# A two-layer network kernel on one core: loads of x moved to another queue in its first stage, loads and first products reordered in its last ones

## What is computed

```python
x = x + _L0_conv_ref(_ln_c(x), ...)   # involution: 7x7 taps, dilation 2, 8 groups, taps made per point from a reduction of _ln_c(x)
t = t + _L0_ffn_ref(_ln_t(t), ...)    # 16 spectral filters; weights of four matrix sets mixed by a softmax of 4 values
x = x + _L1_conv_ref(_ln_c(x), ...)   # 3x3 convolution of rank one, its factors made from means of the image
t = t + _L1_ffn_ref(_ln_t(t), ...)    # 8 experts, the two best of a softmax per point
# _ln_c, _ln_t: (v - mean) / sqrt(var + eps) over the 128 channels of a point
# inside _L0_ffn_ref:
y_soft = softmax(log_weights + gumbel); weights = one_hot(argmax(y_soft)) - y_soft + y_soft
```

## Time and profile before

| what | us |
|---|---|
| median of three runs (2830.85 to 2849.27) | 2848.44 |
| the profiled execution, its own time | 2834.71 |
| its span, first to last instruction | 2832.9 |
| `normalise_in`, to the next block's first GpSimd instruction | 0 to 207.0 |
| `back_and_norm`, first instruction | 2160.5 |
| `experts`, first instruction | 2376.9 |

### The profile page before, as it was taken

The page is one execution under the profiler, slowest core; times in us unless marked ns, Lnnn a source line. Parts: engine busy times, 40 slices in busy tenths (PEclk is TensorE's granted clock), DMA queues, the critical chain, the costliest instruction groups (busy, mean ns, idle before and its releaser), DMA issues. The chain is left out here.

```text
span 2832.9 us, 78733 instructions
## 1 busy us (share of the span) xinstructions
PE 2358.3 (83%) x34528; PEld 1799.9 (64%) x34528; DVE 1495.8 (53%) x3482; ACT 1309.7 (46%) x2623; POOL 366.5 (13%) x651
## 2 busy tenths in 40 slices
PE   3549898768169999999999999999785984799898
PEld 2328898633058888888888888888433751344444
DVE  3852433357136665666566566656211452576777
ACT  3443433356046655665566565656210563333332
POOL 1311111124300000000000000000021001122211
PEclk7676977879689999999999999999897886899999
DMA  6457535365621111111101111110398410000000
GB/s 196 144 138 162 107 82 102 73 216 177 153 77 45 45 45 45 45 45 45 36 23 44 45 45 45 45 23 19 123 298 290 140 55 13 13 20 25 21 24 26
DMA packets 155227, 235.09 MB, mean 83 GB/s; under 512 B 18310, under 2 KB 112623, under 8 KB 151372
## 3 DMA queue, kind: packets, MB, share of 16 engines
q1 hardware_dynamic: 122392, 134.74, 16.4%
q0 software_dynamic: 32496, 95.33, 12.5%
HBM read 141.68 MB, written 88.31 MB: 81 GB/s over the span
## 5 line engine op out<-in xcount | busy, mean ns | idle before, releaser
L1026 DVE COPY spc_g<-spc_pz 128x512 f32<-128x512 f32 x1024 | 629.1, 682 | 306.5 <-PE spc_pz L922 306.5
L996 ACT ACTIVATE spc_g<-spc_pz 128x512 f32<-128x512 f32 x1024 | 549.2, 612 | 284.5 <-PE spc_pz L922 284.1
L922 PE MATMUL spc_pz<-spc_v,spc_as 108*128 108x128 bf16 x8192 | 553.9, 219 | 13.8 <-issue 1.7
L922 PEld LDWEIGHTS spc_pz<-spc_v,spc_as 108*128 108x128 bf16 x8192 | 473.6, 97 | 102.7 <-ACT spc_g L996 31.4
L943 PE MATMUL spc_pz<-spc_g,spc_u 128*20 128x128 f32 x16384 | 469.2, 274 | 21.4 <-DVE spc_g L1026 17.3
L943 PEld LDWEIGHTS spc_pz<-spc_g,spc_u 128*20 128x20 f32 x16384 | 451.4, 134 | 47.5 <-ACT spc_g L996 30.1
L1533 PE MATMUL moe_ex<-moe_ew,moe_d 128*128 128x512 f32 x512 | 249.8, 611 | 32.8 <-DVE moe_yt L1690 32.4
L907 PE MATMUL spc_pu<-spc_f,spc_s 128*128 128x256 f32 x768 | 207.6, 396 | 80.6 <-DMA spc_s<-s_sf 80.6
L1690 DVE SCALAR_TENSOR_TENSOR moe_yt<-moe_ex,moe_gb,moe_yt 128x128 f32<-128x128 f32 x768 | 209.6, 343 | 103.3 <-ACT moe_yt L1592 98.0
L566 DVE SCALAR_TENSOR_TENSOR inv_xo<-inv_pa,inv_mask,inv_xo 128x256 f32<-128x256 f32 x256 | 123.6, 484 | 219.7 <-PE inv_pa L524 187.0
L544 ACT ACTIVATE inv_b<-inv_pb 112x1024 f32<-112x1024 f32 x128 | 125.5, 1021 | 216.8 <-PE inv_pb L503 216.8
(11 more groups left out here) (218 smaller groups left out, 2282.0 us busy)
## 6 DMA issues: line engine op xcount, KB each, us to landing
s_yd<-spc_yo SPq DMA_DIRECT2D x128, 160.0 KB
s_sf<-fwd_so SPq DMA_DIRECT2D x16, 1024.0 KB, 6.4
spc_s<-s_sf POOLq DMA_DIRECT2D x32, 512.0 KB, 6.1
ivs_y<-s_yd POOLq DMA_DIRECT2D x32, 512.0 KB, 5.1
s_td<-ivs_to SPq DMA_DIRECT2D x32, 512.0 KB, 5.3
ln_t<-s_td SPq DMA_DIRECT2D x32, 512.0 KB, 3.9
lnc_xc<-in_x SPq DMA_DIRECT2D x32, 256.0 KB, 5.3
s_xn<-lnc_xn SPq DMA_DIRECT2D x64, 128.0 KB
```

The costliest lines, as they stand in the source:

```text
L922: m = pe.matmul(pz[:, (p + 2) % 3, e // 4, 2 * FT * (e % 4):2 * FT * (e % 4) + 2 * FT], AS[:, x, 8 * p + e, :], V[:, k, x, :, FT * t:FT * ...
L996: act.activation(g_out(p, 0), g_in(p, 0), ACT.Copy).then_inc(ga, 1)
L1026: v.tensor_copy(g_out(p, 1), g_in(p, 1)).then_inc(gd, 1)
```

## The change

In `normalise_in` x gets six buffers, and its loads move from SP's list to GpSimd's, where the other work of that list is put between them. SP's list begins with the small constants and both first matrix sets, and the other sets go out one DMA at a time behind the stores of chunks 3 to 8. The square root, the normalisation, the turning back, the product and its removal move one step later each, the product has four banks, and the weight work lies at other steps. In `back_and_norm` the loads of X of images 1 to 3 wait for units of the image before. In `experts` the first group's neighbour rows are issued first, from GpSimd and ACT, and its products use four banks each and an order of their own.

```diff
-    NQ, D = NB * NCH, 4
+    NQ, D, DX = NB * NCH, 4, 6
-        pr = A.ps("pr", [P, 2, CH])
+        pr = A.ps("pr", [P, 4, CH])
-            for s in range(NQ + 5):
+            for s in range(NQ + 7):
...
+            for q in range(NQ):
+                if q >= DX:
+                    pool.wait_ge(x_turned, q - DX + 1)
+                pool.dma_start(xc[:, q % DX, :], xv[q // NCH, q % NCH]).then_inc(x_in[q % DX], 16)
+                if q == 0:
+                    step(pool.memset(eps[:], EPS_C))
+                if q == 3:
+                    step(pool.memset(zero[:], 0.0))
+                if q in (17, 18):
+                    if q == 17:
+                        pool.wait_ge(mats_used, 4)
+                    combine(q - 17)
+                if 19 <= q < 23:
+                    split(q - 19)
+                if 8 <= q < 17:
+                    store_zeros(q - 8)
+                if q == 24:
+                    pool.wait_ge(wc_ready, 1)
+                    pool.dma_start(S["D2M"], d2[:].rearrange("p a b -> p (a b)")).then_inc(out_done, 16)
+                if q == 26:
+                    store_parts(1)
             store_parts(0)
-            store_parts(1)
...
             sp.dma_start(ident[:], I["ident"]).then_inc(const_in, 16)
-            load_x(0)
+            sp.dma_start(lg[:, 0, :], I["lw"].partition_broadcast(P)).then_inc(small_in, 16)
+            sp.dma_start(lg[:, 1, :], I["gum"].partition_broadcast(P)).then_inc(small_in, 16)
+            sp.dma_start(sg[:, 0, :], I["sigma"].partition_broadcast(P)).then_inc(small_in, 16)
+            sp.dma_start(prio[:], I["prio"]).then_inc(small_in, 16)
             sp.dma_start(wr[:], I["w_reduce"]).then_inc(const_in, 16)
             sp.dma_start(rbias[:], I["b_reduce"]).then_inc(const_in, 16)
...
-            load_mats(0)
+            for i in range(2):
+                for m in range(3):
+                    load_mats(i, m)
             for q in range(NQ):
                 b, n = divmod(q, NCH)
-                if q + D < NQ:
-                    load_x(q + D)
                 sp.wait_ge(xn_ready, q + 1)
...
-                if q in (1, 6, 9):
-                    load_mats((1, 6, 9).index(q) + 1)
+                if 3 <= q < 9:
+                    load_mats(2 + (q - 3) // 3, q % 3)
...
-                if q >= 2:
-                    pe.wait_ge(red_ready, q - 1)
-                pe.matmul(pr[:, q % 2], wr[:], xnc[:, q % 2], start=True, stop=True).then_inc(reduced, 1)
+                if q >= 4:
+                    pe.wait_ge(red_ready, q - 3)
+                pe.matmul(pr[:, q % 4], wr[:], xnc[:, q % 2], start=True, stop=True).then_inc(reduced, 1)
...
-                if live(s - 3):
-                    turn_back(s - 3)
                 if live(s - 4):
-                    reduction(s - 4)
+                    turn_back(s - 4)
+                if live(s - 5):
+                    reduction(s - 5)
...
-                q = s - 1
+                q = s - 2
                 if live(q):
                     act.wait_ge(mv_ready, q + 1)
...
-                q = s - 2
+                q = s - 3
...
-                q = s - 3
+                q = s - 4
...
-                elif s in (5, 8, 11, 14):
-                    add_mats((5, 8, 11, 14).index(s))
-                elif s == 10:
+                elif s in (3, 5, 9, 12):
+                    add_mats((3, 5, 9, 12).index(s))
+                elif s == 7:
                     inverse_weights()
-                elif s in (16, 18):
-                    combine(s // 2 - 8)
-                elif s in (20, 22, 24, 26):
-                    split(s // 2 - 10)
+                elif s in (14, 16):
+                    combine(s // 2 - 7)
+                elif s in (18, 20, 22, 24):
+                    split(s // 2 - 9)
...
-                if live(s - 1):
-                    scales(s - 1)
-                if live(s - 5):
-                    take(s - 5)
+                if live(s - 2):
+                    scales(s - 2)
+                if live(s - 6):
+                    take(s - 6)
...
             for b in range(NB):
+                if b:
+                    pool.wait_ge(x_done, NU * (b - 1) + 2)
                 pool.dma_start(X[:, T * b:T * b + T], S["X1C"][b]).then_inc(x_in[b], 16)
...
+        def conv_at(i, c):
+            return pd[:] if i else ex[:, c]
+
+        def centre_at(i, c):
+            return (pd[:], pf[:, 0], pf[:, 1], pl[:])[0 if i else c]
...
+            sp.dma_start(cmat[:], I["cmat"]).then_inc(early_in, 16)
...
-            pool.memset(eb[:], 0.0).then_inc(set_up, 1)
+            for tap in range(0, 9, 2):
+                neighbour(pool, 0, tap, v9_in[0])
             pool.memset(rw[:], 0.0).then_inc(set_up, 1)
             pool.memset(eps[:], EPS_T).then_inc(set_up, 1)
             pool.memset(onec[:], 0.0).then_inc(set_up, 1)
+            pool.memset(eb[:], 0.0).then_inc(set_up, 1)
...
-            pe.wait_ge(const_in, 16 * (6 + GT))
+            pe.wait_ge(early_in, 80)
+            conv(0, 0)
+            for c in range(1, GC):
+                conv(0, c)
+                centre(0, c - 1)
+            centre(0, GC - 1)
             pe.wait_ge(set_up, 5)
-            for c in range(GC):
-                conv(0, c)
-                centre(0, c)
+            pe.wait_ge(const_in, 16 * (5 + GT))
...
-            act.wait_ge(set_up, 5)
+            for tap in range(1, 9, 2):
+                neighbour(act, 0, tap, early_in)
             for c in range(GC):
                 centred(0, c)
+            act.wait_ge(set_up, 5)
...
-            v.wait_ge(const_in, 16 * (6 + GT))
             for c in range(GC):
                 add_conv(0, c)
+            v.wait_ge(const_in, 16 * (5 + GT))
```

More of the change, by code:

```diff
@@ L145, in store_parts, with split @@
                         "e (k d) -> e k d", k=KX)).then_inc(out_done, 16)
[L147 to L153, removed]
+            def split(k):
+                if k == 0:
+                    step(pool.tensor_copy(parts[:, 1, 0], ab[:, 1]))
+                elif k == 1:
+                    step(pool.tensor_tensor(tmp[:, 1], ab[:, 1], parts[:, 1, 0], ALU.subtract))
+                elif k == 2:
+                    step(pool.tensor_copy(parts[:, 1, 1], tmp[:, 1]))
+                else:
+                    step(pool.tensor_tensor(parts[:, 1, 2], tmp[:, 1], parts[:, 1, 1], ALU.subtract))
+                    pool.sem_inc(parts_ready[1], 1)
@@ new lines, in store_zeros @@
+            def store_zeros(k):
+                if k == 8:
+                    pool.dma_start(S["VP"], zero[0:66, 0:NB * 66].rearrange("h (b w) -> h b w", b=NB)).then_inc(out_done, 16)
+                    return
+                side, k = (0, HP - PADH)[k // 4], k % 4
+                if k == 3:
+                    pool.dma_start(S["XN"][side:side + PADH].rearrange("h x w b y c -> (h x w b y c)").rearrange("(p m) -> p m", m=2048),
+                                   zero[0:PADH * HP, :]).then_inc(out_done, 16)
+                else:
@@ L161, in _ @@
-            split3(pool, ab[:, 1], tmp[:, 1], parts[:, 1, 0], parts[:, 1, 1], parts[:, 1, 2], step)
-            pool.sem_inc(parts_ready[1], 1)
+            xv = I["x"].rearrange("b c (n m) -> b n c m", m=CH)
+            for q in range(NQ):
[19 more added lines that the diff above has]
+                    store_parts(1)
@@ L168, in _, with load_mats @@
         def _(sp):
[L169 to L176, removed]
+            def load_mats(i, m):
                 if i >= 2:
                     sp.wait_ge(mats_used, i - 1)
-                for m, name in enumerate(("Mpp", "Mpm")):
+                if m < 2:
@@ L363, in statistics @@
                     m = v.bn_stats(st[:, q % D, t, :], xt[:, q % D, t, :])
-                m.then_inc(st_ready, 1)
-                v.wait_ge(st_ready, q + 1)
+                step(m)
                 if q >= D:
@@ L1432, in experts, with neighbour @@
         gt_at = pl[:, 0:P]
+        def conv_at(i, c):
+            return pd[:] if i else ex[:, c]
+        def centre_at(i, c):
+            return (pd[:], pf[:, 0], pf[:, 1], pl[:])[0 if i else c]
+        rows = S["VP"].rearrange("h b w -> b h w")
+        def neighbour(eng, i, tap, landed):
+            ti, tj = divmod(tap, 3)
+            r0 = (i % 2) * 32 + ti
+            eng.dma_start(v9[tap:tap + 1, i % 2],
+                          rows[i // 2:i // 2 + 1, r0:r0 + 32, tj:tj + W]).then_inc(landed, 16)
         def by_chunk(a):
@@ L1438, in _ @@
         def _(sp):
-            for dst, src in ((ident[:], I["ident"]), (cmat[:], I["cmat"]), (ew[:], I["expert_w"]), (rb[:], I["router_b"].partition_broadcast(P)), (prio[:], I["prio8"])):
+            sp.dma_start(cmat[:], I["cmat"]).then_inc(early_in, 16)
+            for dst, src in ((ident[:], I["ident"]), (ew[:], I["expert_w"]), (rb[:], I["router_b"].partition_broadcast(P)), (prio[:], I["prio8"])):
                 sp.dma_start(dst, src).then_inc(const_in, 16)
@@ L1477, in _ @@
```

(2 more changed lines are left out.)

77 lines of the change are left out of this document (30 added, 47 removed).

## The result

Twenty runs of the changed kernel have a median of 2806.84 us (2779.65 to 2835.92), twenty of the kernel before 2840.02; the ratio is 0.9874, 95% interval 0.9849 to 0.9899. That is some 36 us faster, just over the 1% that a measurement of this kernel can tell. 62.8 had been forecast: the direction held, and over 40% of the gain is missing.

A forecast was written before the change was run, and what follows sets the result against it. Waits at three places were taken as lost from the whole span, with VectorE's work and DMA as close floors in the first stage. Gains 35.6 + 13.2 + 14.0 = 62.8 gave 2771.9 or 2785.6; forecast 2780 us, range 2748 to 2818.

The forecast's parts named there:

- Second normalisation: Start of `back_and_norm`: PE's 13.2 us wait for the second tile of t goes; 13 us gained, bounds 7 to 16.
- Experts: Start of `experts`: first product 5.6 us earlier, products back to back at 1.85 each; scores 14.0 us earlier, bounds 10 to 16.
- Matrices: First stage: VectorE waits for later matrix sets at steps 9 and 12, 14 us for both, bounds 0 to 35.
- rival A: DMA becomes the first stage's bound, 19.7 MB needed by step 12; gain there 19, total about 2800; chance 25%.
- Last steps: First stage, steps 25 to 30 without weights: PE's or ACT's period counts, 6 x 3.3 = 20 us (2.7 to 3.5 each).
- Tail: First stage, from the last statistics to the next stage's first GpSimd instruction: 15 us with the deeper step, 13.0 before.
- Start: First stage: small inputs land 2.4 us earlier, so the first statistics begin at 10.4 instead of 12.8; bounds 10 to 12.8.
- x six ahead, four banks, aggregates: First stage: nearly all 83 us of x waits go, and the 33.8 for the bank and 13.9 for aggregates go.
- The 13 us beside GpSimd: First stage: VectorE's two-input instructions still stand still some 13 us beside GpSimd's arithmetic; kept, bounds 0 to 20.
- B: Everything uncouples: matrices in time and the higher clock; 85 us less, 2760; chance 12%.
- C: Slower: GpSimd's queue feeds x too slowly in the first stage; at a landing of 50, about 2881; chance 2%.
- D: First stage: waits for x turn into waits for matrices one for one; only 27 us less, 2820; chance 6%.

The follow-up runs named there:

- e9: Changed kernel with chunk stores issued from ACT and all matrix loads in one go from SP; first stage 190.7 us, matrix waits 9.3.
- e3: Changed kernel with the nine border stores behind loads 18 to 26; ratio to the kernel before 0.9882, first stage 192.1 us, matrix waits 17.9.
- e4: Changed kernel without the loads of the third and fourth matrix set, additions kept on the first two sets' data; first stage 175.6 us.
- e6: Changed kernel with the third matrix set issued whole behind the store of chunk 0, the fourth behind that of chunk 4; first stage 183.9 us.
- e8: Changed kernel with all six `s_as` stores held until all chunks but the last are normalised; first stage 196.7 us.
- e10: Changed kernel with GpSimd waiting for the three constants ahead of x(1); first stage 192.5 us, first statistics at 10.99.
- e2: Kernel before with only the two late stages changed, `normalise_in` as before; ratio to the kernel before 0.9941.
- e5: Changed kernel with a fifth buffer for the normalised chunks; first stage 196.7 us.
- e7: Changed kernel with borders behind loads 18 to 26, sets whole behind stores 0 and 4, five output buffers; ratio to before 0.9839, first stage 182.0 us.
- e12: Changed kernel run once more, unchanged; ratio to the kernel before 0.9858, median 2808.91 us, first stage 192.2 us.
- e11: Changed kernel with late borders, sets issued whole early and five output buffers, run again; ratio to before 0.9799, median 2801.74 us, first stage 181.6.

## Why the prediction was right and wrong

**The late stages: right, in part by luck.** *Second normalisation*: no hole, first unit 11.2 us after the block's beginning (11.0 before). The clock's rise to the upper level, which the forecast had feared to leave where it was, came with PE's unbroken work (that the one brought the other was not tried apart): in before the stretch of 60 to 70 us into the stage is the first with a clock of 1.00, in after that of 50 to 60. -12.7 against -13.2. That it came so close is luck: with the new loads the stage took 201.2 to 206.6 us in seven profiles and 211.9 to 212.5 in five, where the old ones took 216.3 and 215.6, so the gain was 4 us in the five and lay under the bound of 7 (last section). *Experts*: first product 7.2 us after the beginning instead of 5, the steps between products 2.0 rather than 1.85, scores at 23.7, 11.5 earlier than before rather than 14.0. The stage as a whole gained 13.6; the last 2.1 us come behind the scores, and what gave them wasn't tried. This gain is steady: 442.4 to 444.8 us in twelve profiles with the new order, 456.0 and 456.6 with the old.

**The first stage: the mechanism right, two terms mis-sized and two missing.** Step by step, forecast and measured:

| term | forecast | measured |
|---|---|---|
| first statistics | 10.4 | 13.10 |
| steps 0 to 24 without matrix waits | 112 | 108.15 |
| matrix waits at steps 3 and 5 | 0 | 9.32 |
| matrix waits at steps 9 and 12 | 14 | 18.31 |
| steps 25 to 31 | 20 | 25.70 |
| tail | 15 | 18.86 |
| sum | 171.4 | 193.44 |

(Step 25's statistics begin at 148.88, and 148.88 - 13.10 - 9.32 - 18.31 = 108.15; the last begin at 174.58.)

*Matrices* is the step that failed, twice. The larger part of the miss lies at *steps 3 and 5*, for which the sum had nothing: the first two sets cost 2.57 + 6.75 = 9.32. There the DMA engines are full (10 to 30 us), e9 keeps 9.3 of it with no store in SP's way, and e3, without the borders, still has 2.1 + 2.9. That points at bandwidth; but SP issues the second set behind the first, with issues of up to 7.42 us, and no run moved bytes away from these two sets alone, so what bounds them isn't fully shown. At *step 9* the forecast took the store behind which a part stands to be issued when its data are ready, and "up to 3 us of issue and 9.0 to land". In truth SP was behind by itself: parts 2 and 3 of the second set held it until 30.1, and the stores between the later parts took 7.4 and 7.8 us to issue. The wait was 15.43, where the sum had 4.3 to 7.3, although the last part landed sooner than assumed, after 5.5. At *step 12* SP was not behind: the store of chunk 8 went out at 76.50, just when its data were there (ACT's instructions end at 76.48), the last part landed within 6.1, and the wait was 2.88, under the 5.7 to 8.7 of the sum. So 14 and 18.31 lie near each other by luck: one wait was priced far too low and the other too high.

Long issues could be read from the trace of before. There too SP took long over chunk stores soon after the border stores (27 to 34 us) and after the `s_as` stores (163 to 170), 10.84 us for one pair and 10.07 for a single store, and 4.55 for one part of 1 MB:

```profile
39.03 10.84 SPq L204 DMA_DIRECT2D s_xn<-lnc_xn  x2
...
174.91 10.07 SPq L204 DMA_DIRECT2D s_xn<-lnc_xn  x1
```

e4 prices the two later sets at 17.8 us, e6 gets 9.5 of it back by order alone, and e3 finds 10 us of waits in the borders' company; so rival A, the early 19.7 MB, fits steps 3 and 5 and was not the bound at 9 and 12, since in e9 the two later sets are there in time with the same bytes, at 283 GB/s over the first 66 us (254 in after).

*Last steps.* Without the waits the step is 2.69 us (171.89 to 174.58), the good end of the stated 2.7 to 3.5. But 8.26 and 0.82 us of waiting for ACT stand among them, and behind these ACT's wait of 8.04 for a chunk store beside the `s_as` stores. The chunk stores are late already at their issue: single ones took SP 6.57 us at 131.60 and 5.83 at 154.50. The forecast had seen that x suffers beside these stores and not that the chunk stores do; before, ACT waited for no chunk store. e8 shows it: without that company the last statistics are 11.7 earlier. *Tail*: 5.9 more than before (13.0), where 2 had been allowed for the deeper step. The last normalisation begins 7.7 us behind the last statistics (4.3 before), and from the issue of its last store at 185.1 to the end it is 8.3 (6.6 before). The `s_as` stores had landed long since (the last, issued at 149.5, within 13.2), and what delays this last store was not tried.

*Start.* The last of the small inputs came at 8.5 rather than 5.8 (8.2 - 2.4), beside the six x loads (shown by e10). *x six ahead, four banks, aggregates*: right, the waits are zero. *The 13 us beside GpSimd*: right; two 128x4 operations took 3.1 us, a copy of 128x128 4.45, and with three more such instructions it is 14.4 over what their fellows take. *GpSimd's list*: PE waited for no x. Of its issues of x none took over 0.81 us, and the 2.69 of the earlier trace rows didn't recur, so GpSimd's stall beside VectorE, priced at 5 us in the prediction, cost nothing that these rows show.

**Rivals.** A held half, as said, and its 2800 was the nearest to the median. In part that is the measure: the kernel before has a median of 2840 in twenty runs, not 2848, and by the gain the 36 us lie between A's 46 and D's 27. B fell: ACT's pace was there, the matrices weren't in time. C and D fell: the stage did shorten, and not one for one with what x had cost.

## What to carry to other kernels

When a queue's list is ordered, a load's time of issue is the sum of what stands ahead of it in that list, with the issue times that the list has when it is loaded; walk the whole list, with the longest issue times that the old trace shows beside such transfers, and don't count back from the data it waits for. Taking one wait away speeds up every producer, so ask which stores and buffers were never late only because everything was slow. And where the untouched stages of two profiles differ by as much as the change, compare the touched stages with each other and leave the total to the runs.

## What was unexpected of the hardware

In after, one DMA's issue on SP took 0.4 us at the start and up to 7.4 us behind the matrix loads: `lnc_mp` from 0.71 to 7.42, `s_xn` from 0.50 to 7.06. On ACT's queue a single chunk store took up to 5.92 (e9). Before the change SP had such issues too, of up to 10.07 us for one chunk store.

`back_and_norm` with the new loads, the same code in all of them, shows two lengths: 201.2 to 206.6 us in after, e2, e4, e5, e7, e8 and e12, and 211.9 to 212.5 in e3, e6, e9, e10 and e11. Its stretches differ in the granted clock alone (PE busy 158.1 us at 0.79 against 167.1 at 0.76):

```profile
2158.80:2362.80 204.00, 158.09 (x752) 106.07 (x752) 91.69 (x172) 103.64 (x136) 8.07 (x18) 0.79 0.40 125
```

```profile
2143.20:2355.70 212.50, 167.05 (x752) 111.04 (x752) 91.69 (x172) 103.64 (x136) 8.11 (x18) 0.76 0.39 120
```

The first is after, the second e11. In e11 and e3 the clock fell to about 0.66 some 90 us into the stage, after 30 us at the upper level, where in after it stayed at 0.87 or higher from 50 to 120 us; e8, at 206.6, has the same fall and a higher clock later on. What decides between the two was not found, and at some 8.5 us it is worth most of the 12.7 that the stage's new order brings.
